# Second-layer experts by dispatch, with the routing inside the attention and all loops written out

## The chip, the cores and the metric

One core of a Trainium2 chip runs the whole program in a single launch. Five instruction streams work side by side and meet only at semaphores: TensorE (PE: matmuls and transposes), VectorE (DVE), ScalarE (ACT), GpSimd (POOL) and SyncE (SP), which issues the DMA transfers. The metric is the device time of one execution in microseconds; lower is better. All data is float32.

## The reference

Two transformer layers over x of 2 batches x 1024 tokens x 128 channels. Each layer is a gated attention and a gated feed-forward block, each behind a modulated layer norm. The parts that matter for the change are in the second layer:

```python
h = _layernorm(x) * (1 + ca) + sa
x = x + ga * _L1_attn_ref(h, Wq, Wk, Wv, Wo)       # linear attention, 16 heads of 32, sequences of 128
h = _layernorm(x) * (1 + cb) + sb
x = x + gb * _L1_ffn_ref(h, gate_w, w1, w2, w3)

def _L1_ffn_ref(x, gate_w, w1, w2, w3):            # E = 8 experts, 4 of them masked out, K = 2, H = 704
    logits = where(expert >= 4, -inf, xf @ gate_w.T)
    top_w, top_idx = top_k(softmax(logits), 2)
    cw[token, top_idx] = top_w / sum(top_w)
    h = silu(xf @ w1[e]) * (xf @ w3[e])            # for every expert e
    out = sum_e cw[:, e] * (h_e @ w2[e])
```

So four experts are live, and each token uses two of them. The first layer has another attention and 16 experts of hidden width 256 of which each token uses one. x lies in the core's own memory as `x_sb`, 16 tiles of 128 tokens x 128 channels.

## The kernel before

The program is a sequence of phases, each of which ends with all engines meeting: setup, `rwkv_phase` (first attention, eight chunk steps, to about 225 us), `expert_phase` (first experts, to about 358 us), `hla_phase` (second attention, to about 679 us), `swiglu_phase` (second experts, to the end). Within a phase each engine runs a hand-written order of instructions, and semaphore counts tie the engines together.

`rwkv_phase`, `expert_phase`, `hla_phase` and `swiglu_phase` each hold a hardware loop (`Fori`) on every engine: three passes of two chunk steps in the first; four rounds of eight slot tiles in the second; six chunks in the third (`steps`, L1289 to L1300: chunk 0 and chunk 7 are written out beside the loop); four groups of 512 tokens in two loop passes or rounds in the fourth.

The first layer's experts go by dispatch. The token rows are written into slots sorted by expert (POOL's indirect DMA, L1010), SP reads 32 expert numbers into registers with `value_load` (L965) and fetches each slot tile's weights; the results go to DRAM (`slots_out`, L977) and POOL gathers them back (L1017).

`hla_phase` works in 64 units: 8 chunks of 128 tokens x 2 batches x 4 groups of heads. Per unit PE projects q, k, v (L1323 to L1325), transposes (L1338, L1339, L1343), and runs many 32-row products (L1361 to L1424); DVE makes `h_aT` (L1496), updates the state (L1499) and masks the products (L1505); ACT evicts. Every fourth unit carries an output projection. POOL adds the gated output into `x_sb` (L1521, L1524).

`swiglu_phase` starts when the attention is done. A preamble computes the layer norm, the transposed tokens, the logits, the softmax (ACT L1699), the top two (DVE L1754, L1757) and the weights of all tokens. Then all four experts are computed for every token: per group of 512 tokens 22 units (a block of 128 hidden channels of one expert, or two tails of 64), each of two up products (L1659, L1661), ACT's silu (L1716), DVE's product (L1784) and one down product (L1669). A token that doesn't use an expert enters it with weight zero: POOL scales the rows (L1811), PE transposes them (L1645), and these scaled tokens are the input of the w3 product. The result is transposed back (L1688), multiplied by the gate (L1788), added to `x_sb` (L1827) and stored from there (L1835).

## Time and profile before

| | us |
|---|---|
| median of 3 runs | 972.87 |
| lowest and highest | 969.47 and 982.83 |
| the profiled execution | 969.88 |
| its span in the trace | 968.1 |
| PE busy in it | 771.0 |
| DVE busy | 403.2 |
| ACT busy | 296.2 |
| POOL busy | 185.3 |

The profile is one execution on the core. A timeline row gives start and length in us, engine, line of the kernel, operation, output<-inputs, and in brackets the engine's idle time ahead of the row with what ended it; "issue" means that it waited for nothing that the profile shows. A float32 matmul appears as two entries (two passes), so a row with x4 holds two matmuls of the program. PEclk is the TensorE clock that was granted, as a share of full speed. Starts of matmuls are measured, their ends are modelled: the distance from one start to the next is the safer price.

### The profile page before, as it was taken

The numbers are of one execution on the slowest core, as the hardware profiler recorded it, in microseconds if no ns is written. First come the engines' busy times: TensorE is split into PE (matmuls) and PEld (weight loads), VectorE is DVE, ScalarE is ACT, GpSimd is POOL, SyncE is SP. The second block draws the span as 40 slices with busy tenths as digits, with TensorE's granted clock in tenths as the row PEclk, the third lists the DMA queues.
The fourth block names the chain that finished last, engine by engine and source line by source line (L and its number), as shares of the span: only waits on it lengthen the run. The fifth ranks groups of instructions, "written<-read, shape, count | busy, mean of one in ns | idle before, by whom it ended". The sixth has DMA issues, their size and how long they took to land. (4 is left out here: it accounts for less than half of the span.)

```text
span 968.1 us, 25870 instructions
## 1 busy us (share of the span) xinstructions
PE 771.0 (80%) x10310; PEld 542.1 (56%) x10310; DVE 403.2 (42%) x1126; ACT 296.2 (31%) x903; POOL 185.3 (19%) x285
## 2 busy tenths in 40 slices
PE   4777777744178329999898988999459999999997
PEld 4455555434067318887787877887424444444442
DVE  4366777752222254453443534444522222222221
ACT  0343444321034114443343333443122222322221
POOL 1245445431500350000000100000221010110100
PEclk8587878755579759999999999999559999999999
DMA  5700000002356200000000000000000000000000
GB/s 141 223 3 2 0 0 0 0 2 88 123 160 220 86 21 3 3 4 3 4 3 3 3 4 4 3 3 3 1 0 1 0 12 0 12 0 0 11 0 11
DMA packets 27296, 28.11 MB, mean 29 GB/s; under 512 B 3200, under 2 KB 20288, under 8 KB 27200
## 3 DMA queue, kind: packets, MB, share of 16 engines
q1 hardware_dynamic: 26176, 24.58, 8.2%
q0 software_dynamic: 1024, 2.10, 0.7%
q8 instruction: 79, 1.29, 0.6%
q14 instruction: 17, 0.14, 0.0%
HBM read 20.38 MB, written 6.29 MB: 28 GB/s over the span
## 5 line engine op out<-in xcount | busy, mean ns | idle before, releaser
L1505 DVE TENSOR_TENSOR h_masked<-quad,const 128x1536 f32<-128x1536 f32 (+2 forms) x66 | 112.8, 1709 | 141.7 <-PE quad L1367 134.6
L1659 PE MATMUL quad<-f_xg,moe_w 128*128 128x512 f32 x320 | 152.5, 602 | 0.8 <-ACT f_xg L1704 0.8
L1784 DVE TENSOR_TENSOR f_h<-f_sa,quad 128x512 f32<-128x512 f32 x88 | 60.6, 688 | 181.1 <-PE quad L1659 164.8
L1659 PEld LDWEIGHTS quad<-f_xg,moe_w 128*128 128x128 f32 x320 | 60.2, 193 | 70.0 <-issue 69.5
L1716 ACT ACTIVATE f_sa<-quad 128x512 f32<-128x512 f32 x88 | 52.5, 597 | 143.8 <-PE quad L1659 126.7
L1669 PE MATMUL bank<-f_h,moe_w 128*128 128x512 f32 x160 | 82.5, 597 | 0.0
L1521 POOL TENSOR_TENSOR h_added<-h_added,mod_row 128x128 f32<-128x128 f32 x16 | 7.3, 455 | 285.0 <-ACT h_added L1472 285.0
L1669 PEld LDWEIGHTS bank<-f_h,moe_w 128*128 128x128 f32 x160 | 29.7, 190 | 40.9 <-issue 40.9
L1476 ACT ACTIVATE h_gT<-bank 128x128 f32<-128x128 f32 x64 | 17.7, 277 | 113.9 <-PE bank L1410 112.4
L1361 PE MATMUL quad<-h_qk 32*128 32x128 f32 x1024 | 48.9, 307 | 0.0
L1323 PE MATMUL pair<-h_hT,hla_wq 128*128 128x128 f32 x128 | 32.0, 333 | 20.1 <-issue 16.4
L1452 ACT ACTIVATE h_qk<-pair 128x256 f32<-128x256 f32 x64 | 24.5, 383 | 71.3 <-PE pair L1325 71.3
L1361 PEld LDWEIGHTS quad<-h_qk 32*128 32x128 f32 x1024 | 36.1, 194 | 10.4 <-issue 8.6
L1811 POOL TENSOR_TENSOR g_hs<-g_h_all,g_cw 128x512 f32 (+1 forms) x20 | 20.6, 1040 | 93.2 <-PE pair L1645 71.8
L631 POOL TENSOR_TENSOR kl<-kl,tot 128x128 f32<-128x128 f32 x56 | 26.9, 481 | 45.1 <-DVE state L575 17.2
L1827 POOL TENSOR_TENSOR x_sb<-x_sb,f_gated 128x512 f32 x4 | 5.1, 1265 | 155.9 <-DVE f_gated L1788 155.9
L1323 PEld LDWEIGHTS pair<-h_hT,hla_wq 128*128 128x128 f32 x128 | 19.6, 192 | 24.5 <-issue 18.1
L1496 DVE TENSOR_TENSOR h_aT<-bank,const 128x128 f32<-128x128 f32 x64 | 18.7, 291 | 31.7 <-PE bank L1424 29.1
L1381 PE MATMUL bank<-h_qk,h_state 32*32 32x128 f32 x512 | 28.1, 291 | 0.0
L1402 PE MATMUL bank<-h_masked,h_vt 128*32 128x128 f32 x512 | 27.8, 290 | 0.0
L1017 POOL DMA_INDIRECT e_yt<-slots_out,slot_of_token x16 | 15.6, 976 | 63.0 <-DMA slots_out<-e_yg 58.4
L1224 PE MATMUL quad<-const,h_all 128*128 128x128 f32 x16 | 4.0, 423 | 29.5 <-DVE h_all L1153 29.5
(285 smaller groups left out, 1673.5 us busy)
## 6 DMA issues: line engine op xcount, KB each, us to landing
e_w<-in_experts_dram SPq DMA_DIRECT2D x32, 257.5 KB
moe_w<-in_moe_w_dram SPq DMA_DIRECT2D x2, 1408.0 KB, 9.3
slots_in<-zero SPq DMA_DIRECT2D x4, 512.0 KB, 4.0
e_xg<-slots_in SPq DMA_DIRECT2D x8, 256.0 KB, 3.2
slots_out<-e_yg SPq DMA_DIRECT2D x8, 256.0 KB, 4.6
moe_w<-in_moe_w_dram SPq DMA_DIRECT2D x4, 320.0 KB, 7.2
x_sb<-in_L_attn_x_dram SPq DMA_DIRECT2D x2, 512.0 KB, 8.4
out_dram<-x_sb SPq DMA_DIRECT2D x4, 256.0 KB, 2.4
```

The costliest lines, as they stand in the source:

```text
L631: pool.tensor_tensor(halves(kl[m + 1], m)[:, :, 0], halves(kl[m], m)[:, :, 0], per(tot[m], m)[:, :, 1:2].to_broadcast([P, N >> (m + 1), 1 ...
L1323: pe.matmul(proj[:, 0:P], W["q"][:, cols], hT[b][:, :], start=True, stop=True)
L1361: last = pe.matmul(quad[:, h, a * P:(a + 1) * P], qk[q][head(h), 1 - a, :], qk[q][head(h), a, :], start=True, stop=True, tile_position=(h ...
L1381: pe.matmul(left[head(h), 0:P], states[k][head(h), 2 * D:3 * D], qk[k][head(h), 1, :], start=True, stop=False, tile_position=(h * D, h * D ...
L1402: last = pe.matmul(left[head(h), 0:P], vt[k][:, head(h)], new[:, h, P:2 * P], start=False, stop=True, tile_position=(0, h * D), skip_group ...
L1452: act.activation(qk[q][:, :, :], proj[:, 0:2 * P].rearrange("p (k n) -> p k n", k=2), ACT.Copy).then_inc(s_qkv, 1)
L1505: dve.tensor_tensor(masked[k % 4][:, :, a * P:z * P], quad[:, :, a * P:z * P], cst("causal")[:, None, a * P:z * P].to_broadcast([P, HPG, ( ...
L1659: return pe.matmul(dst[:, :], w[:, e, f * P:(f + 1) * P], src(e), start=True, stop=True)
L1669: pe.matmul(acc[b][:, :], w, hh[n % 2][:, :], start=(n == 0), stop=(n == U - 1))\
L1716: act.activation(sa[n % 2][:, :], up_a[n % 2][:, :], ACT.Silu).then_inc(s_sa, 1)
L1784: dve.tensor_tensor(hh[n % 2][:, :], sa[n % 2][:, :], up_b[n % 2][:, :], ALU.mult)\
L1811: pool.tensor_tensor(hs[k % 2][:, :, :], h_all[:, bass.ds(at + k, 1), :].to_broadcast([P, E, C]), cw[:, 0, bass.ds(at + k, 1), :].rearrang ...
```

## The change

1. `hla_phase` and `swiglu_phase` become one `layer1_phase`. The second layer's experts are computed only for the tokens that use them. Each token's row is written to two slots (`moe1_slots` in DRAM, one region for each expert). A row is a payload of 132 numbers: 128 channels of the normalised token, the token's number, the weight, the batch and a spare. 4096 rows in four regions fill at most 35 tiles of 128 slots.
2. The routing of chunk m runs inside the attention on its way through chunks m + 1 and m + 2, one part a unit (`routed`): DVE's stats, centre, normalise, logits, top2, ranked, slots and weights; two 8-column matmuls on PE (`rank`); an Exp on ACT (`weigh`); POOL's deviation, logit products, payload copy and four indirect scatters (`send`). There are two payload buffers, used in turn. Chunk 7's routing comes after the attention. Its gate rows are made ahead of the attention: a load, matmuls on PE, a copy on ACT.
3. SP stores each finished chunk of `x_sb` to a DRAM accumulator `moe1_acc`.
4. DVE computes from the four counts the tables `expert_of` and `row_of`; PE reads 35 expert offsets into registers, once; SP reads 5 row numbers a round.
5. Seven rounds of five tiles. A tile: SP loads 128 payload rows; PE transposes them, three up products (512, 512 and 384 columns: w1 and w3 side by side), six transposes of the hidden rows, six down products of 128 columns, with w addressed through the register; ACT three silus and two copies; DVE three products, a copy and the weighting; POOL picks the gate row by batch (three operations) and scatters with an add into `moe1_acc`. Each scatter waits until the one before it has landed.
6. At the end SP copies 1 MB from `moe1_acc` to the output.
7. In the phases of layer 0 and in the attention the hardware loops are replaced by loops that are written out when the program is built. A fill of `moe1_slots` (4.5 MB, constant) and another layout of the expert weights are loaded during `rwkv_phase`.

The diff, cut to its core:

```diff
-            with eng.Fori(0, CHUNKS - 2) as n:
+            for n in range(0, CHUNKS - 3):
                 for k in range(PER):
-                    step(n + 1, k)
+                    step(n + 2, k)
...
+        def routed(i, k, at):
+            if k % PER != at:
+                return None
+            m = i + k // PER - (1 if at >= 3 else 2)
+            return m if not isinstance(m, int) or m >= 0 else None
...
+            def rank(m, first):
+                pe.wait_ge(r_ohs, m + 1)
+                pe.wait_ge(r_cum, m * 2 + 1)
+                pe.matmul(right[:, 232:240], cst("before"), ohs[:, :, :]...
+                pe.matmul(right[:, 232:240], cst("ones"), cum[:, :, :]...
...
+            def expert(n):
+                return pe.value_load(expert_of[0:1, bass.ds(n, 1)], min_val=0, max_val=(E - 1) * EXPERT1)
+            turn(0, 0)
+            experts = [expert(n) for n in range(TILES1)]
+            ups(0, 0, 0, experts[0])
...
+            def down(i, k, e):
+                pe.wait_ge(f_mostc, tile(i, k) + 2)
+                pe.wait_ge(f_restc, tile(i, k) + 2)
+                pe.wait_ge(f_y, tile(i, k) + (1 if k else 2))
+                for f in range(FULL1):
+                    pe.matmul(acc[k % 2], hidT[k][:, f * P:(f + 1) * P],
+                              W2[:, bass.ds(e + (2 * F1 + f * C), C)], start=(f == 0), stop=False)
...
+            def round_(i, last):
+                for k in R:
+                    ups(i, k, 2, es[k])
+                    turn_most(i, k)
+                    turn(*((i, k + 2) if k + 2 < U else (i + 1, k + 2 - U)))
+                    ups(j, q, 0, es[k + 1])
+                    turn_rest(i, k)
+                    ups(j, q, 1, es[k + 1])
+                    down(i, k, es[k])
...
+            def step(i, k):                                             # VectorE
+                dve.tensor_tensor(aT[q][:, :], right[:, 0:P], ...
+                m = routed(i, k, 2)
+                if m is not None:
+                    ranked(m)
+                dve.scalar_tensor_tensor(out=states[q][:, :], ...
+                if m is not None:
+                    slots(m)
+                    weights(m)
+                for at, part in ((3, stats), (4, centre), (5, normalise), (7, logits), (0, top2)):
+                    m = routed(i, k, at)
+                    if m is not None:
+                        part(m)
+                dve.tensor_tensor(masked[k % 4][:, :, a * P:z * P], ...
...
+            def scatter(i, k):
+                pool.wait_ge(f_y, n + 2)
+                pool.wait_ge(f_add, n * 16)
+                pool.indirect_dma_start(out=t["moe1_acc"], ..., in_=yg[k][:, :], compute_op=ALU.add)\
+                    .then_inc(f_add, 16)
...
+            sp.wait_ge(f_add, 16 * TILES1 + 16)
+            sp.dma_start(out..., t["moe1_acc"][0:BATCH * SEQ, :]...).then_inc(f_out, 16)
```

DVE's order in the attention before, at the head of the loop (L1295 is the loop's own): `h_aT`, `h_state` and `h_masked` follow each other, with nothing between them but the loop's register arithmetic.

```order
L1295 UNCONDITIONAL_BRANCH
L1295 ISA
L1496 TENSOR_TENSOR h_aT<-bank,const 128x128
L1499 SCALAR_TENSOR_TENSOR h_state<-h_state,bank 128x96
L1504 REGISTER_ALU
L1505 TENSOR_TENSOR h_masked<-quad,const 128x1536
L1495 REGISTER_ALU
```

The same place now, the unit of a chunk that holds `top2`, from the end of the unit ahead of it:

```order
L1829 TENSOR_TENSOR h_aT<-bank,const 128x128
L1835 SCALAR_TENSOR_TENSOR h_state<-h_state,bank 128x96
L1781 MAX g_mx<-g_lg 128x8 x2
L1785 MAX_INDEX g_idx<-g_mx,g_lg 128x8 x2
L1786 TENSOR_TENSOR g_gap<-g_mx 128x2
L1788 CAST g_idf<-g_idx 128x4
L1790 TENSOR_TENSOR g_oh<-const,g_idf 128x16
L1794 TENSOR_TENSOR g_ohs<-g_oh 128x8
L1796 TENSOR_TENSOR g_cum<-g_cum,g_ohs 128x4
L1848 TENSOR_TENSOR h_masked<-quad,const 128x1536
```

Nine instructions (MAX and MAX_INDEX are two each) have moved in between the state and the mask; two units later the unit with `ranked`, `slots` and `weights` holds seven more, of which the first stands between `h_aT` and `h_state`.

PE's order in the second layer's experts before, at the head of the loop: up products of 512 tokens and one down product per block of 128 hidden channels.

```order
L1651 UNCONDITIONAL_BRANCH
L1651 ISA
L1654 ISA
L1674 ISA
L1659 MATMUL quad<-f_xg,moe_w 128x512 x2
L1674 REGISTER_ALU
L1659 MATMUL quad<-f_xg,moe_w 128x512 x2
L1668 REGISTER_ALU
L1669 MATMUL bank<-f_h,moe_w 128x512
```

PE's order there now, from chunk 7's rank and the counts (`g_cum`) over the first transposed tile of payload rows (`f_xg`) to the first of 35 register loads:

```order
L1513 MATMUL bank<-g_cum,const 128x8
L1566 MATMUL bank<-g_cum,const 128x4
L1585 MATMUL pair<-const,f_xg 128x128
L1625 TENSOR_LOAD g_expert_of
L1625 ISA x2
```

and the middle of one tile (`h_masked` is the memory that now holds the hidden rows; ISA rows are register arithmetic for an address):

```order
L1593 ISA
L1593 MATMUL quad<-moe_w,f_xT 128x384
L1601 MATMUL quad<-const,h_masked 128x128 x4
L1585 MATMUL pair<-const,f_xg 128x128
L1593 ISA
L1593 MATMUL quad<-moe_w,f_xT 128x512
L1608 MATMUL pair<-const,h_masked 128x128 x2
L1593 ISA
L1593 MATMUL quad<-moe_w,f_xT 128x512
L1617 ISA
```

followed by the six down products, each behind an ISA row of its own. The loads stand behind a transpose that waits for the first payload tile, and seven transposes of 128 columns stand among three wide products.

## Rows read from the trace of the kernel before

**Rows 1.** Windows: PE, PEld, DVE, ACT, POOL busy us (x), granted clock, DMA share, GB/s
```profile
50.00:150.00 100.00, 76.92 (x1017) 52.14 (x1015) 69.26 (x253) 39.72 (x133) 48.54 (x82) 0.83 0.00 1
...
500.00:680.00 180.00, 165.76 (x4074) 143.49 (x4066) 78.23 (x103) 66.15 (x257) 12.18 (x27) 0.97 0.01 3
680.00:700.00 20.00, 9.68 (x46) 9.34 (x47) 13.29 (x65) 2.39 (x4) 5.15 (x8) 0.53 0.01 1
...
720.00:840.00 120.00, 118.65 (x313) 51.35 (x311) 30.98 (x45) 31.59 (x53) 8.53 (x9) 0.99 0.01 3
```

**Rows 2.** Timeline of PE, second experts: the first product, and three rows in the middle
```profile
716.85 1.22 PE L1659 MATMUL quad<-f_xg,moe_w 128*128 128x512 f32 x1 [0.76 <-ACT f_xg L1704]
...
880.32 1.88 PE L1659 MATMUL quad<-f_xg,moe_w 128*128 128x512 f32 x4
882.04 1.02 PE L1669 MATMUL bank<-f_h,moe_w 128*128 128x512 f32 x2
```

**Rows 3.** Timeline of PE: first and last of five loop edges in the attention
```profile
437.82 0.37 PE L1323 MATMUL pair<-h_hT,hla_wq 128*128 128x128 f32 x1 [3.05 <-issue]
...
601.11 0.37 PE L1323 MATMUL pair<-h_hT,hla_wq 128*128 128x128 f32 x1 [3.53 <-issue]
```

**Rows 4.** Timeline of DVE in the attention, the mask of three units in a row
```profile
622.80 1.76 DVE L1505 TENSOR_TENSOR h_masked<-quad,const 128x1536 f32<-128x1536 f32 x1 [1.61 <-PE quad L1367]
...
627.06 1.76 DVE L1505 TENSOR_TENSOR h_masked<-quad,const 128x1536 f32<-128x1536 f32 x1 [1.61 <-PE quad L1367]
...
632.22 1.76 DVE L1505 TENSOR_TENSOR h_masked<-quad,const 128x1536 f32<-128x1536 f32 x1 [2.51 <-PE quad L1367]
```

**Rows 5.** Timeline of PE, first layer: the same transpose in four steps
```profile
105.35 0.44 PE L743 MATMUL quad<-const,xn 128*128 128x128 f32 x2 [2.48 <-DVE xn L448]
...
126.98 0.44 PE L743 MATMUL quad<-const,xn 128*128 128x128 f32 x2 [2.53 <-DVE xn L448]
...
149.69 0.44 PE L743 MATMUL quad<-const,xn 128*128 128x128 f32 x2 [2.48 <-DVE xn L448]
```

**Rows 6.** Timeline of PE: 128-column matmuls late and at the start of the attention
```profile
601.43 0.39 PE L1324 MATMUL pair<-h_hT,hla_wk 128*128 128x128 f32 x2
601.65 0.39 PE L1325 MATMUL pair<-hla_wv,h_hT 128*128 128x128 f32 x2
...
360.60 0.64 PE L1324 MATMUL pair<-h_hT,hla_wk 128*128 128x128 f32 x2
361.03 0.64 PE L1325 MATMUL pair<-hla_wv,h_hT 128*128 128x128 f32 x2
```

**Rows 7.** Timeline of POOL: the last write of the attention into x_sb
```profile
678.39 0.45 POOL L1524 TENSOR_TENSOR x_sb<-x_sb,h_added 128x128 f32<-128x128 f32 x1
```

**Rows 8.** Value loads: DVE's table, SP's first load after it, and line 965 by source
```profile
248.82 0.17 DVE L1107 TENSOR_SCALAR expert_of_tile<-r_te 1x32 int32<-1x32 f32 x1
...
254.03 4.62 SPq L969 DMA_DIRECT2D e_w<-in_experts_dram  x8
...
L965 SPq TENSOR_LOAD <-expert_of_tile x32: 261/263/677, 249.0 to 305.8; - x32
```

**Rows 9.** Timelines of POOL and SP: the last two scatters, and the load behind them
```profile
266.42 0.96 POOL L1010 DMA_INDIRECT slots_in<-h_all,slot_of_token  x1 [0.31 <-issue]
267.69 0.96 POOL L1010 DMA_INDIRECT slots_in<-h_all,slot_of_token  x1 [0.30 <-issue]
...
269.93 6.89 SPq L973 DMA_DIRECT2D e_xg<-slots_in  x3
```

**Rows 10.** Page, parts 6 and 3: DRAM transfers to landing, and instruction fetch
```profile
slots_out<-e_yg SPq DMA_DIRECT2D x8, 256.0 KB, 4.6
...
out_dram<-x_sb SPq DMA_DIRECT2D x4, 256.0 KB, 2.4
...
q8 instruction: 79, 1.29, 0.6%
```

**Rows 11.** Page, part 5: the product on DVE in the last stage
```profile
L1784 DVE TENSOR_TENSOR f_h<-f_sa,quad 128x512 f32<-128x512 f32 x88 | 60.6, 688 | 181.1 <-PE quad L1659 164.8
```

More of the change, by code:

```diff
@@ L428, in steps @@
             step(0, 0, True, False)
-            with eng.Fori(0, CHUNKS // 2 - 1) as j:
+            for j in range(0, CHUNKS // 2 - 1):
                 step(j * 2 + 1, 1, True, True)
@@ L985, in _ @@
                 load_x(s, 0)
-            with sp.Fori(0, ROUNDS - 1) as i:
+            for i in range(0, ROUNDS - 1):
                 experts = experts_of(i + 1)
@@ L1036, in _ @@
                 act.sem_inc(s_out[s], 16)
-            with act.Fori(0, ROUNDS) as i:
+            for i in range(0, ROUNDS):
                 for k in range(DEPTH):
@@ L1113, in _ @@
             dve.wait_ge(s_exp, 3)
-            with dve.Fori(0, ROUNDS) as i:
+            for i in range(0, ROUNDS):
                 def inputs(half):
@@ L1184, in _ @@
                       stop=True).then_inc(s_rank, 1)
-            with pe.Fori(0, ROUNDS) as i:
+            for i in range(0, ROUNDS):
                 def transposes(half):
@@ L1441, in _ @@
             steps(pe, step)
+            pe.wait_ge(r_place, (CHUNKS - 2) * 2 + 1)
+            rank(CHUNKS - 1, True)
+            pe.wait_ge(r_cum, CHUNKS * 2)
+            pe.matmul(left[:, 256:256 + E], cst("ones"), cum[:, 0, :], start=True, stop=True).then_inc(s_cnt, 1)
+            pe.wait_ge(s_w2, 16 * S_W2)
+            pe.wait_ge(r_place, (CHUNKS - 1) * 2 + 1)
+            pe.sem_inc(f_hh, 3)
+            pe.sem_inc(f_mostc, 1)
+            pe.sem_inc(f_restc, 1)
+            pe.sem_inc(f_y, 2)
@@ new lines, in turn_most, with turn_rest @@
+            def turn_most(i, k):
+                pe.wait_ge(f_hh, tile(i, k) * 3 + 5)
+                pe.wait_ge(f_mostc, tile(i, k) + 1)
+                for f in range(4):
+                    last = pe.transpose(most[:, f * P:(f + 1) * P], hh[k][:, f * P:(f + 1) * P], cst("ident"))
+                last.then_inc(f_most, 1)
+            def turn_rest(i, k):
+                pe.wait_ge(f_hh, tile(i, k) * 3 + 6)
+                pe.wait_ge(f_restc, tile(i, k) + 1)
+                for f in range(2):
+                    last = pe.transpose(rest[:, f * P:(f + 1) * P], hh[k][:, (4 + f) * P:(5 + f) * P], cst("ident"))
+                last.then_inc(f_rest, 1)
@@ new lines, in _ @@
+            dve.wait_ge(s_tab, 10)
+            dve.scalar_tensor_tensor(out=rt[:, :], in0=te[:, :], scalar=float(CAP1 // P), in1=bt[:, :], op0=ALU.mult,
+                                     op1=ALU.subtract).then_inc(s_tab, 1)
+            dve.wait_ge(s_tab, 11)
+            dve.tensor_tensor(rt[:, :], rt[:, :], cst("iota35")[0:1, :], ALU.add).then_inc(s_tab, 1)
+            dve.wait_ge(s_tab, 12)
+            dve.tensor_scalar(row_of[:, :], rt[:, :], float(P), None, ALU.mult).then_inc(s_table, 1)
@@ new lines, in round_ @@
+            def round_(i, last):
+                for k in R:
+                    hidden(i, k, 2)
+                    j, q = (i, k + 1) if k + 1 < U else (i + 1, 0)
+                    keep_rest(i, k)
+                    if not last or k + 1 < U:
+                        hidden(j, q, 0)
+                        hidden(j, q, 1)
+                    result(i, k)
+            hidden(0, 0, 0)
+            hidden(0, 0, 1)
+            round_(0, False)
+            for n in range(0, ROUNDS - 2):
+                round_(n + 1, False)
@@ new lines, in _, with chunk @@
+            pool.wait_ge(s_growc, 1)
+            pool.wait_ge(s_fill, 16)
+            pool.dma_start(t["moe1_acc"][BATCH * SEQ:BATCH * SEQ + P, :], blank[:, 0:C]).then_inc(f_add, 16)
+            def chunk(i, first=2, last=False):
+                if first >= 1:
+                    add(i - 1, 1)
+                if not last:
+                    pool.wait_ge(s_proj, i * PER + GROUPS)
+                    fetch(i + 1, 0)
+                if first >= 2:
+                    send(i - 2)
+                if first >= 1:
+                    deviation(i - 1)
+                    products(i - 1)
+                    payload(i - 1)
+                add(i, 0)
+                if not last:
+                    pool.wait_ge(s_proj, i * PER + 2 * GROUPS)
+                    fetch(i + 1, 1)
```

696 lines of the change are left out of this document (418 added, 278 removed).

## The prediction

> **What bounds the kernel now.** I read the windows first, to see which engine is full in which stretch. In the second attention PE is busy 165.8 of 180 us at a granted clock of 0.97, and in the second experts 118.7 of 120 at 0.99, while no other engine is busy for half of the time [rows 1]. PE is the bound of both stages. Between them, 680 to 700, it is busy half of the time at the lower level: there the span is set by the preamble's chain. Next I read PE's timeline of the experts: two up products (x4) start 1.72 us before what follows, so a pass of 512 columns costs 0.43 us and a matmul 0.86 [rows 2]. This stage runs from 716.85 to the end, 251.3 us. The preamble lasts from the last write into x_sb, which ends at 678.84 [rows 7], to 716.85: 38.0 us. Last, PE's timeline of the attention. PE stood idle 3.05 and 3.53 us, for "issue", ahead of the first and the last of five loop edges [rows 3]; nothing that the profile shows was awaited.
>
> **The attention's loop edges.** From the first edge to the last are four passes in 163.3 us, 40.8 each [rows 3]. Without an edge a chunk is six units of 4.26 and two with the output projection of 5.16, by the distances of DVE's masks [rows 4]: 35.9. So an edge costs 4.9: the idle 3 to 3.5, and a slower unit behind it. Five edges: **-24.7**. The instruction fetch moved 1.29 MB in all [rows 10]; at 64 bytes each, my assumption, that is about PE's 20,000 entries, so the loop's body was already fetched pass by pass, and writing it out needs no more of it per us.
>
> **The first layer's loops.** One transpose starts at 105.35, 126.98 and 149.69: 21.63 without and 22.71 with an edge between [rows 5], so 1.1 for each of three edges, **-3.2**. The first experts' rounds have three edges too; no row isolates one there. Bounds 0 and 5 us, I take 1 each: **-3**. The 4.5 MB fill is issued early in the first layer, where nothing waits for DMA (DMA share 0.00) [rows 1]; if that cover went, it is about 15 us at the 2 MB in 6.6 that the zero fill of the first experts needs by its issues; I cost it at nothing.
>
> **Gate rows ahead of the attention.** A small load that lands in about 2.4 [rows 10], four matmuls at the lower clock and an ACT copy come before PE's first projection: **+4** (bounds 2 and 7).
>
> **Routing in the attention.** PE gains two logical matmuls of 8 columns a chunk with their waits; their cost is at most that of two 128-column ones, 0.22 each at full clock [rows 6]: +3.5. ACT must change its table for the first Exp; no table load is in the rows, bounds 0.3 and 3, I take 1.3. On DVE the nine instructions of top2 are the longest insertion, 0.17 each by the shortest DVE row [rows 8] and up to 0.25, so 1.5 to 2.2. They stand ahead of a mask that waits 1.61 us for PE, 2.51 in units with the projection [rows 4]. That covers almost all. What is late if not is the mask, then the products behind it; the state and `h_aT` follow. I take +1 in all, and 0 and 12 as bounds: 12 is 0.2 of a us in each of 60 units. Sum of this part **+5.8**. POOL's five operations and four sends a chunk, under 12 us, lie in 36 us of a POOL that was busy 12.2 of 180 [rows 1].
>
> **From the attention's end to the first up product.** Chunk 7's routing is serial: some 30 dependent DVE, POOL, PE and ACT operations of 0.17 [rows 8] to 0.45 [rows 7], 9.4 us. Then four sends 1.27 apart [rows 9]; the last is issued at 13.3. The last scatter of the first layer was issued at 267.69 and the load that needs all of them at 269.93 [rows 9], so it landed within 2.24: 15.5. The load of the first payload tiles and its landing, 2.4 to 4.6 for larger ones [rows 10]: 19. On PE the transpose of that tile stands ahead of the 35 register loads, so they start only then. SP read eight in the 5.0 us from the table (248.99) to its first load (254.03) [rows 8]: 0.62 each, of which TENSOR_LOAD is 0.26. 35 x 0.62 = 21.7. First up product at 41 instead of 38.0: **+3** (bounds -10, if PE reads in 0.26, and +6).
>
> **The tiles.** Per tile PE runs 1408 columns of up products, 2.35 us by 0.86 per 512 [rows 2]; seven transposes, one pass each, at 0.11, 0.77; six down products of two passes, 1.34 [rows 6]. Together 4.46 us. The nine address instructions have no row on PE. Lower bound 0 each (they are read ahead), upper bound 0.15, about half of what a value load costs beside its TENSOR_LOAD [rows 8]; I take 0.05, nearest to the loop's register arithmetic, which stood between products that followed at 0.43 a pass [rows 2]. So 4.9 a tile, 35 tiles 171.5. DVE's three products of 192 to 256 columns are at most half of 0.69 each [rows 11], with copy and weighting under 1.9; ACT about 2; POOL three of 0.45 [rows 7] and 0.96 [rows 9]: none comes near 4.9. Beyond that 3 at the lower clock after the 21 us of loads, 4 to fill and for stray bubbles, and 11 for the end: weighting, scatter to landing (3), and the 1 MB copy (7; bounds 3 and 12 from 4.6 and 2.4 for a quarter of it [rows 10]). 189.5 against 251.3: **-61.8**.
>
> This needs the full clock. In the attention, which has three transposes a unit, 0.97 was granted; in the first layer, with PE busy 76.9 of 100 us, 0.83 [rows 1]. At 0.83 a tile is 4.46 / 0.83 + 0.44 = 5.8, and the run is 31 us longer. I keep 4.9, because the tiles keep PE as busy as the attention does. The Trainium skill speaks against that: TensorE: Matmul & The Clock Gate, Part 4, says that the clock gate doesn't engage for transposes, since they don't count as PE-busy in the same way. By that rule seven transposes, 0.77 of each tile's 4.9 us, would not count, and the tile would be as the one at 0.83; the attention's rows don't show such an effect.
>
> **The sum.** 968.1 - 24.7 - 3.2 - 3 + 4 + 5.8 + 3 - 61.8 = 888.2 of span. The profiled execution was 969.88, 1.8 above its span, and the median of the runs 3.0 above that: 890 to 893, so **892 us**.
>
> **The rivals.**
> - *Lower clock in the tiles*, as just worked out: 5.8 a tile, 923 us. If PE stays at the lower level altogether, as between 680 and 700 (0.53) [rows 1], a tile is 8.9 and the run 140 longer, about 1030. Against it: PE has work queued throughout. 0.12 and 0.04.
> - *The chain of scatters*. Each waits for the landing of the one before it. A plain scatter takes up to 2.24 to land [rows 9]. With the add its target must be read too: 2.24 + 2.4 = 4.6 hides in 4.9. With the 4.6 of a write to DRAM [rows 10] plus about 1, 5.6 a tile: 35 x 0.7 = 25 more, 916 us. 0.18.
> - *The other side: scatters with add above 7.2*. The rest of the change saves 18, and the tiles with start and end may take 251 + 18, so the run is slower than before from (269 - 18) / 35 = 7.2 a tile, and over 2% slower from 7.7. It needs an add that goes row by row; at 9 it is 1035 us. Nothing in the rows speaks for it but that no accumulating transfer is among them. 0.06.
> - *Register-addressed matmuls bound by PE's sequencer*: at 0.15 for each address and another 0.07 for the second pass's, 5.8 to 6.5 a tile, 923 to 948 us. 0.15.
> - *The dispatch gives nothing and only the edges count*: its tiles at 7, gains 20: about 955. 0.04.
>
> **How the numbers follow.** My forecast (4.5 to 5.3 a tile) gets 0.41. It spans 862 (4.46 a tile and cheap loads) to 908. The range of all goes to 946, which takes in the scatter chain, the clock at 0.83 and most of the sequencer's case, and leaves out about 0.17. A measurement of this kernel can tell about 2% from no change, 19 us, so faster means below 953: 0.41 + 0.12 + 0.18 + 0.15 = 0.86. Slower is 0.04 + 0.06 = 0.10. The last case, at 950 or a little more, is the 0.04 for the same.
>
> **What would show it.** Attention: no idle "issue" ahead of projections, chunks of 36 to 37 us; if DVE binds, PE waits for the mask. Preamble: 35 loads on PE in about 21.7 us. Tiles: down products of successive tiles 4.9 apart with a granted clock near 1. If scatters bind, POOL's come evenly and PE waits for a copy behind `f_y`. If addresses bind, PE idles between down products with nothing awaited. The end: one copy of about 7 us. I would be wrong above all if a tile is not 4.9: each 0.1 is 3.5 us.

## The result

| | before | changed |
|---|---|---|
| median, us | 971.25 (4 runs) | 940.51 (4 runs) |
| lowest and highest | 969.47 and 982.83 | 932.72 and 945.68 |
| profiled execution | 969.88 | 932.72 |
| its span | 968.1 | 930.9 |

The ratio of the changed kernel to the kernel before is 0.965, with a 95% interval from 0.955 to 0.976. So the change makes the kernel 31 us faster. I had forecast 892, which is 81 us faster than the median of 972.87 known then. The direction was right, and 940.51 still lies in the range of 862 to 946, but the gain is 31 us and not 81. Medians here and below are over all executions; two of the kernels below have one execution over 1.5% above their fastest (`e5_fill_split` 935.36, `e9_lazy_loads` 922.76), and without it their medians are 922.02 and 907.17. The stages of the two profiled executions show where it went:

| stage | before | changed | difference | forecast |
|---|---|---|---|---|
| start to the attention's first projection | 360.1 | 375.0 | +14.8 | -2.2 |
| attention, to the end of its last write to x_sb | 318.7 | 326.6 | +7.8 | -18.9 |
| from there to the first up product | 38.0 | 42.0 | +4.0 | +3 |
| second experts, to the end | 251.3 | 187.4 | -63.9 | -61.8 |
| span | 968.1 | 930.9 | -37.2 | -79.9 |

The part of the prediction on the new stages, the last two rows, is within about 2 us in each. The part on the old stages, in which loops were written out and some work was put in, is 44 us off.

First the windows of the changed kernel's profile, with the columns of [rows 1]: most of the first layer's attention, the second attention, and the second experts.

```profile
50.00:200.00 150.00, 119.96 (x1466) 80.69 (x1466) 95.74 (x349) 54.42 (x182) 67.51 (x117) 0.72 0.06 13
374.00:702.00 328.00, 314.28 (x7260) 268.28 (x7260) 174.88 (x384) 123.25 (x472) 73.61 (x113) 0.96 0.04 11
743.00:920.00 177.00, 174.99 (x874) 113.25 (x874) 65.77 (x175) 65.03 (x174) 88.28 (x136) 0.99 0.19 25
```

The reader should see three things. The experts run at a granted clock of 0.99, and PE is busy for 99% of the time. POOL is busy for half of the time there, where it was busy for 7% in the second experts before [rows 1], and doesn't bind. The first layer's attention was granted 0.72 from 50 to 200, where the kernel before was granted 0.82 in the same window.

The tiles, in the timelines of PE and of POOL: the down products of two tiles in a row, and the scatters of these tiles.

```profile
908.52 1.34 PE L1617 MATMUL bank<-moe_w,h_masked 128*128 x10
...
909.79 0.48 PE L1620 MATMUL bank<-moe_w,h_masked 64*128 x2
...
910.21 0.91 PE L1593 MATMUL quad<-moe_w,f_xT 128*128 x2
910.96 0.60 PE L1601 MATMUL quad<-const,h_masked 128*128 128x128 f32 x4
...
913.34 1.34 PE L1617 MATMUL bank<-moe_w,h_masked 128*128 x10
```

```profile
911.40 1.60 POOL L2050 DMA_INDIRECT moe_acc<-f_y,f_token  x1 [2.25 <-DVE f_y L1916]
...
916.22 1.57 POOL L2050 DMA_INDIRECT moe_acc<-f_y,f_token  x1 [2.13 <-DVE f_y L1916]
```

These two are 4.82 apart; in the middle of the stage a tile takes 4.92, by PE's transposes (L1585):

```profile
803.07 0.27 PE L1585 MATMUL pair<-const,f_xg 128*128 128x128 f32 x1
808.00 0.27 PE L1585 MATMUL pair<-const,f_xg 128*128 128x128 f32 x1
```

POOL waits over 2 us ahead of each scatter, for DVE's result of this tile and not for the scatter ahead. The last scatter with add and the copy of 1 MB to the output stand in the list of DMA issues of the last 13 us (the last number is us from issue to landing). The median of all 35 scatters is 3.3, so the chain of scatters has room within 4.92:

```profile
moe_acc<-f_y,f_token POOLq DMA_INDIRECT x1, 3.2
out_dram<-moe_acc SPq DMA_DIRECT2D x1, 5.1
```

The attention. Each chunk from the third on has one unit of 7.4 to 9.2 us, where a unit takes 4.26 [rows 4]. Here is the fourth of the six, around 587. First PE, then POOL, ACT and DVE, each on its own timeline.

```profile
582.38 0.49 PE L1429 MATMUL pair<-h_hT,hla_wq 128*128 128x128 f32 x2
...
587.36 0.24 PE L1545 MATMUL bank<-h_vt,h_kqt 128*32 128x32 f32 x8
...
588.09 0.39 PE L1431 MATMUL pair<-hla_wv,h_hT 128*128 128x128 f32 x2
...
590.44 0.58 PE L1473 MATMUL quad<-h_aT,h_qk 32*128 32x128 f32 x8 [0.65 <-DVE h_aT L1829]
```

```profile
587.30 1.10 POOL L1980 DMA_INDIRECT moe_slots<-g_pay,g_slot  x1 [0.17 <-issue]
588.70 0.97 POOL L1980 DMA_INDIRECT moe_slots<-g_pay,g_slot  x1 [0.30 <-issue]
589.98 0.96 POOL L1980 DMA_INDIRECT moe_slots<-g_pay,g_slot  x1 [0.30 <-issue]
591.24 0.96 POOL L1980 DMA_INDIRECT moe_slots<-g_pay,g_slot  x1 [0.30 <-issue]
```

```profile
591.55 0.38 ACT L1664 ACTIVATE h_qk<-pair 128x256 f32<-128x256 f32 x1 [3.82 <-DMA slots_in<-zero]
```

```profile
590.10 0.29 DVE L1829 TENSOR_TENSOR h_aT<-bank,const 128x128 f32<-128x128 f32 x1 [2.86 <-remote]
...
593.18 1.76 DVE L1848 TENSOR_TENSOR h_masked<-quad,const 128x1536 f32<-128x1536 f32 x1 [1.89 <-remote]
```

DVE's `h_aT` waits for PE's L1545, which by its row was over at 587.60. DVE starts at 590.10. ACT waits for L1431, over at 588.48, and starts at 591.55. So up to there PE's matmuls stand in the trace at their usual distances, but those who wait for PE start 2.5 to 3.1 us late. (The names of the releasers there, a DMA of an earlier phase and "remote", are those of semaphores used again; they are not to be trusted.) It begins with POOL's four payload scatters and ends with them. PE itself then waits, for `h_aT` first, and behind that three times for "issue", 0.17, 0.42 and 0.34 us; all six long units have such waits at the same place, and `e3_loads_first` below, which has no long unit, has none. As the ends of matmuls are modelled, the trace can't tell whether PE's signals come late or the work behind them. The next projection is at 595.97, 8.4 us behind the one at 587.54.

The second stretch that I missed, the first layer's attention: the same transpose as in [rows 5] in two pairs of steps, and PE's longest wait for issue between the first two.

```profile
40.18 0.41 PE L766 MATMUL quad<-const,xn 128*128 128x128 f32 x2 [1.52 <-DVE xn L471]
...
48.36 0.49 PE L819 MATMUL pair<-rl,kl 64*32 64x32 f32 x29 [2.69 <-issue]
...
63.68 0.41 PE L766 MATMUL quad<-const,xn 128*128 128x128 f32 x2 [2.19 <-DVE xn L471]
...
130.88 0.41 PE L766 MATMUL quad<-const,xn 128*128 128x128 f32 x2 [2.42 <-DVE xn L471]
...
157.01 0.49 PE L766 MATMUL quad<-const,xn 128*128 128x128 f32 x2 [2.19 <-DVE xn L471]
```

The second step, 40.18 to 63.68, takes 23.5 us; before it took 18.6 (42.43 to 61.06). The sixth, from 130.88, takes 26.1 where [rows 5] has 21.6 and 22.7. From the first transpose of these steps to the eighth are 155.7 us, against 146.0 before; 4.9 of the 9.7 more stand in the second step, 6.8 in the five behind it, and the first is 2.0 shorter.

Between attention and experts the chain is as forecast, with the loads one block:

```profile
701.08 0.45 POOL L1949 TENSOR_TENSOR x_sb<-x_sb,h_added 128x128 f32<-128x128 f32 x1
```

```profile
720.17 0.47 PE L1585 MATMUL pair<-const,f_xg 128*128 128x128 f32 x1 [8.99 <-DMA f_xg<-moe_slots]
743.50 2.07 PE L1593 MATMUL quad<-moe_w,f_xT 128*128 x2 [22.85 <-issue]
```

### The profile page after: what moved, and what is told of

Read it like the earlier page. It is cut to its first block, busy times and chain, and to the rows that moved or that the text cites. A ratio compares the mean times of both kernels' runs of the same rounds, so it can differ in the third digit from the quotient of the medians.

```text
span 930.9 us, 26177 instructions
## 1 busy us (share of the span) xinstructions
PE 719.1 (77%) x10523; PEld 555.1 (60%) x10523; DVE 431.1 (46%) x1331; ACT 289.4 (31%) x967; POOL 306.2 (33%) x476
## 4 chain that ended last, share of the span: by engine, by line
PE 50%; issue 4%; DVE 2%; another core or an unknown queue 2%; DMA 1%; POOL 1%; ACT 0%; POOLq 0%; SPq 0%; DVEq 0%; PEldq 0%
PE quad L1593 10%; PE bank L1617 4%; PE quad L1467 4%; PE bank L1493 3%; PE pair L1429 3%; PE bank L1487 3%; PE bank L1520 2%; PE quad L1473 2%; PE quad L1601 2%; PE pair L1454 2%; PE bank L1620 2%; PE pair L1430 2%; PE pair L1431 2%; PE bank L1525 2%; PE bank L1537 2%
## 5 line engine op out<-in xcount | busy, mean ns | idle before, releaser
L1593 PE MATMUL quad<-moe_w,f_xT 128*128 x210 | 105.5, 585 | 22.9 <-issue 22.9
L2050 POOL DMA_INDIRECT moe_acc<-f_y,f_token x35 | 55.6, 1589 | 108.4 <-DVE f_y L1916 105.9
L1904 DVE TENSOR_TENSOR h_masked<-f_sa,quad 128x256 f32<-128x256 f32 (+1 forms) x105 | 41.5, 395 | 80.2 <-ACT f_sa L1712 80.2
L1712 ACT ACTIVATE f_sa<-quad 128x256 f32<-128x256 f32 (+1 forms) x105 | 38.4, 366 | 127.0 <-PE quad L1593 121.2
L1617 PEld LDWEIGHTS bank<-moe_w,h_masked 128*128 128x128 f32 x350 | 41.7, 191 | 22.2 <-issue 22.2
L1593 PEld LDWEIGHTS quad<-moe_w,f_xT 128*128 128x128 f32 x210 | 32.4, 194 | 28.9 <-issue 24.8
L1617 PE MATMUL bank<-moe_w,h_masked 128*128 x350 | 47.1, 281 | 0.7 <-DVE h_masked L1908 0.7
L1467 PEld LDWEIGHTS quad<-h_qk 32*128 32x128 f32 x1024 | 36.2, 187 | 10.7 <-issue 8.7
L1829 DVE TENSOR_TENSOR h_aT<-bank,const 128x128 f32<-128x128 f32 x64 | 18.6, 291 | 48.5 <-PE bank L1545 30.5
L1980 POOL DMA_INDIRECT moe_slots<-g_pay,g_slot x32 | 32.1, 1003 | 11.0 <-issue 8.7
L2039 POOL TENSOR_TENSOR f_gsel<-f_gdiff,f_xg 128x128 f32<-128x128 f32 x35 | 33.3, 952 | 0.0
L614 POOL TENSOR_TENSOR xx<-xx,hT 128x256 f32<-128x256 f32 x40 | 24.3, 636 | 16.4 <-DVE xx L487 16.4
```

The costliest lines, as they stand in the source:

```text
L1467: last = pe.matmul(quad[:, h, a * P:(a + 1) * P], qk[q][head(h), 1 - a, :], qk[q][head(h), a, :], start=True, stop=True, tile_position=(h ...
L1593: pe.matmul(up[u][:, 0:w], xT[k][:, :], W2[:, bass.ds(e + u * 4 * P, w)], start=True, stop=True).then_inc(f_up, 1)
L1617: pe.matmul(acc[k % 2], hidT[k][:, f * P:(f + 1) * P], W2[:, bass.ds(e + (2 * F1 + f * C), C)], start=(f == 0), stop=False)
L1712: act.activation(sa[u][:, 0:WIDTH[u]], up[u][:, 0:WIDTH[u]], ACT.Silu).then_inc(f_sa, 1)
L1904: dve.tensor_tensor(hh[k][:, at:at + w], sa[u][:, 0:w], up[u][:, w:2 * w], ALU.mult).then_inc(f_hh, 1)
L1980: pool.indirect_dma_start(out=t["moe1_slots"], out_offset=bass.IndirectOffsetOnAxis(ap=slot[:, b * 2 + k:b * 2 + k + 1], axis=0), in_=pay[ ...
```

## The experiments

The runs fell on two chips, which I call chip 1 and chip 2; the chip of the first result is not known. The kernel before takes about the same on both (970.26 to 973.13 us on chip 1, 973.48 on chip 2). Stage times are from each run's profiled execution, as above. "Attention" is from the first projection to the end of the last write to `x_sb`, 318.7 in the kernel before and 326.6 in the changed kernel.

### Does the burst of scatters hold up PE?

`e1_no_send` leaves out the scatters of chunks 0 to 5, so most tiles compute on blank rows. The waits for these scatters are left out too (not shown).

```diff
-                for b in range(BATCH):
+                for b in range(BATCH if m >= CHUNKS - 2 else 0):
```

> Leaves out the payload scatters of chunks 0 to 5 (24 of 32 indirect DMAs of POOL in the attention; the tiles then compute on blank rows). In the changed kernel one unit of every chunk from chunk 2 on takes 7.4 to 9.2 us instead of 4.26, and it begins when POOL issues its four scatters. Theory A (the scatters hold up PE's semaphores or work): these six units go back to 4.26 to 5, the attention gets 25 to 28 us shorter, the run is about 905 to 915. Rival B (instruction fetch for the written-out code, or SP's 64 KB store of the chunk that starts at the same time): the units stay at 7.4 to 9.2 and the run within 5 us of the changed kernel.

`e2_spread` keeps all four and issues them one at a time, between POOL's other work of the chunk.

```diff
-                    send(i - 2)
+                    send(i - 2, (0,))
                 deviation(i - 1)
+                    pool.wait_ge(s_proj, i * PER + 7)
+                    send(i - 2, (1,))
                 products(i - 1)
                 payload(i - 1)
+                    send(i - 2, (2,))
                 add(i, 0) ... fetch(i + 1, 1)
                 ...
+                    send(i - 2, (3,))
```

> The same scatters, but one each in units 3, 4, 6 and 8 of a chunk instead of four in a row. Theory A1 (only a burst of scatters holds PE up, a single one finds slack): the long units shrink to under 5 us and the run is 20 to 28 us faster than the changed kernel, about 912 to 920. Theory A2 (each scatter costs PE about 1.2 us wherever it stands): four units a chunk of about 5.4, the sum stays, run within 5 us of the changed kernel. Rival B as before: one unit a chunk stays at 7.4 to 9.2.

On chip 2 the first took 910.85 us (909.23 to 914.12) and the second 912.51 (902.18 to 914.56), and neither has a long unit: the attention is 298.7 and 298.6. That looked like theory A. But two other kernels measured with them, `e3_loads_first` and `e4_rwkv_loop` (below), keep the burst of four and have no long unit either. Their attention is 298.7 and 298.1. PE's projections there, in `e3_loads_first`, and the burst beside them:

```profile
570.30 0.49 PE L1429 MATMUL pair<-h_hT,hla_wq 128*128 128x128 f32 x2
574.56 0.49 PE L1429 MATMUL pair<-h_hT,hla_wq 128*128 128x128 f32 x2
```

```profile
570.05 1.10 POOL L1980 DMA_INDIRECT moe_slots<-g_pay,g_slot  x1 [0.17 <-issue]
571.46 0.97 POOL L1980 DMA_INDIRECT moe_slots<-g_pay,g_slot  x1 [0.30 <-issue]
572.73 0.96 POOL L1980 DMA_INDIRECT moe_slots<-g_pay,g_slot  x1 [0.30 <-issue]
```

The same burst at the same place of the unit, and the unit takes 4.26. So these four runs couldn't tell what the burst does in the changed kernel. I ran that again, unchanged.

> The changed kernel itself, unchanged, in more executions and perhaps on another chip. Of four variants, three kept its bursts of scatters or its written-out code as they were and none had a long unit in the attention. Theory A (a burst of four scatters holds PE up by itself) then needs the long units back here: about 933 to 945 us. Theory E (the hold-up isn't of the program but of the execution or the chip): no long units, attention about 300 us instead of 326.6, and 905 to 920 us. Theory F (the exact placement of the program matters, which every edit shifts): the long units come back here and in no variant.

On chip 1: 940.47 us (938.02 to 944.61), six long units of 7.0 to 9.4, attention 326.4. Theory E or F was left: the chip or the occasion, or the placement of the program. The next pair decided it.

> The changed kernel once more, beside the variant with the loads first, on one chip. So far all bursts with long units ran on one chip (and on the unknown one of the first result), and the bursts without long units on another. Theory E (the chip decides): both kernels of this pair, which have the same bursts, behave alike: both have long units (attention about 327 us), or neither has (about 299). Theory F (the placement of the program decides): this one has them, the other doesn't, whatever the chip.

> The other of the pair: the loads ahead of the first transpose, bursts as in the changed kernel. Theory E: as its partner, with or without long units. Theory F: no long units while its partner has them.

Both fell on chip 1. The changed kernel took 939.85 and has the long units, attention 327.8. `e3_again`, the very kernel that had none on chip 2, took 931.43 and has them too: six of 8.2 to 9.1, attention 326.6. Theory E: it is not the program's placement. All runs on chip 2 were made on one occasion, so the chip itself and that occasion aren't told apart; on chip 1 the burst had its long units on all three occasions. One more pair, on chip 1 again, asks whether the burst is needed there.

> One scatter each in four units instead of four in a row, and nothing else. On the chip where the changed kernel has its long units: if a burst is what it takes (theory A1), none of 7 to 9 us is left and the attention takes 299 instead of 327; if each scatter costs its share (A2), four units a chunk are 1 us longer. On a chip without long units it tells nothing new: 299.

> Two bursts of two scatters a chunk, about two and a half units apart. If PE falls behind with every scatter that follows another one closely, each pair costs 1 to 2.5 us, together about half of the burst of four: attention about 312. If the slack of a unit covers a pair: 299. On a chip without long units: 299 either way.

`e8_pairs` is as `e2_spread`, with `send(i - 2, (0, 1))` behind the fetch and `send(i - 2, (2, 3))` behind the products. `e2_again` took 913.82 us: no long unit, attention 299.6. SP's store of each chunk (rival B) is still there, so it isn't the cause. `e8_pairs` took 924.35 in its one run, attention 308.4, where I expected 312. Its PE and POOL:

```profile
588.45 0.49 PE L1429 MATMUL pair<-h_hT,hla_wq 128*128 128x128 f32 x2
593.97 0.49 PE L1429 MATMUL pair<-h_hT,hla_wq 128*128 128x128 f32 x2
598.24 0.49 PE L1429 MATMUL pair<-h_hT,hla_wq 128*128 128x128 f32 x2
```

```profile
588.19 1.07 POOL L1981 DMA_INDIRECT moe_slots<-g_pay,g_slot  x1 [0.16 <-issue]
589.57 0.97 POOL L1981 DMA_INDIRECT moe_slots<-g_pay,g_slot  x1 [0.30 <-issue]
```

The unit with the pair takes 5.52, the next 4.27. The chunk's second pair falls into a unit with an output projection, which takes 5.62 to 5.65 instead of 5.16. So on chip 1 a scatter that stands alone costs PE nothing, a pair 1.3 or 0.5 us, and four in a row 3 to 5. On chip 2 four in a row cost nothing. What differs between the two, and what in the chip makes those who wait for PE start late, these runs don't show. PE's waits for "issue" in the long units leave the supply of its instructions as one untested candidate.

### What lengthens the first layer's attention?

`e5_fill_split` cuts the fill of the slots (8576 packets of 528 bytes, the 4.5 MB of the change's list) into seven DMAs, one behind each step. POOL's wait for the fill is adapted (not shown).

```diff
-            sp.dma_start(t["moe1_slots"].rearrange("(q p) n -> p q n", p=P),
-                         blank[:, None, :].to_broadcast([P, SLOTS1 // P, PAY])).then_inc(s_fill, 16)
+            rows = t["moe1_slots"].rearrange("(q p) n -> p q n", p=P)
+            for n in range(7):
+                a, z = n * 10, min(n * 10 + 10, SLOTS1 // P)
+                sp.wait_ge(s_state, 3 * (n + 1))
                 ...
+                sp.dma_start(rows[:, a:z, :], blank[:, None, :].to_broadcast([P, z - a, PAY])).then_inc(s_fill, 16)
```

> The 4.4 MB fill of the slots, which the changed kernel issues in one DMA at the start, is cut into seven pieces, one behind each step of the first layer's attention. In the changed kernel the second step took 23.5 us where the kernel before took 18.6, with 2.7 us in which PE waited for issue while the fill's packets ran. Theory G (the fill holds up PE's instruction fetch): the second step falls to 18 to 20, the run gets 3 to 5 us faster. Rival: the later steps each lose what the second gains, no difference.

Measured on chip 1 beside `after_again`: 925.07 us (920.78 to 935.36) against 940.47. The second step takes 18.4 instead of 27.4, by the same transposes:

```profile
43.64 0.66 PE L770 MATMUL quad<-const,xn 128*128 128x128 f32 x2 [1.50 <-DVE xn L475]
...
62.08 0.41 PE L770 MATMUL quad<-const,xn 128*128 128x128 f32 x2 [2.19 <-DVE xn L475]
```

PE's wait for issue is gone, and the later steps didn't lose it again: 146.7 us from first to eighth instead of 166.3. The other profiles say the same of the second step. All eleven with the whole fill have one wait for issue of 2.0 to 2.8 us while the fill's packets run, and a second step of 23.4 to 27.8 us; the four with the split fill have no such wait, and 18.4 to 18.8.

The gain of 15 is three times what I expected. Of the 19.6 us between the two profiles, 9.0 stand in the second step and 10.7 in the five behind it. Those go together with the clock: by the record of the granted clock, from the first of these steps to 20 us behind the start of the eighth, PE was at the lower of its two levels (1.2 of 2.4 GHz) for 76 us in `e5_fill_split` and for 132 in `after_again`; in the kernel before for 72, in the first result for 104. Over these four profiles the phase is the longer, the more of it is at the lower level: 146.7, 166.3, 146.0, 155.7. Part of that is chance: the three profiles of the unchanged new kernel have 155.7, 159.7 and 166.3. Which of the two, the longer steps or the lower clock, brings on the other isn't shown.

The transposes of the next five steps in `e5_fill_split`, which has no loop edge:

```profile
83.53 0.41 PE L770 MATMUL quad<-const,xn 128*128 128x128 f32 x2 [2.43 <-DVE xn L475]
...
106.24 0.41 PE L770 MATMUL quad<-const,xn 128*128 128x128 f32 x2 [2.43 <-DVE xn L475]
...
127.73 0.41 PE L770 MATMUL quad<-const,xn 128*128 128x128 f32 x2 [2.44 <-DVE xn L475]
...
150.34 0.41 PE L770 MATMUL quad<-const,xn 128*128 128x128 f32 x2 [2.43 <-DVE xn L475]
...
171.90 0.41 PE L770 MATMUL quad<-const,xn 128*128 128x128 f32 x2 [2.42 <-DVE xn L475]
```

From 62.08 on these are steps of 21.4, 22.7, 21.5, 22.6 and 21.6. The kernel before, with its loop, has 21.6, 22.7, 21.6, 22.7 and 21.6. So the alternation of 21.63 and 22.71, which I had read as a step without and a step with an edge [rows 5], is there without any edge. `e4_rwkv_loop` (next), with its edges at the same steps as the kernel before, has it the other way round: 22.8, 21.7, 22.8, 21.7, 22.7.

`e4_rwkv_loop` puts the hardware loop back in this phase alone, and `e6_three` and `e7_four` are a pair that differ by the same edit.

```diff
-            for j in range(0, CHUNKS // 2 - 1):
+            with eng.Fori(0, CHUNKS // 2 - 1) as j:
```

> Only the first layer's attention gets its hardware loop back. From its first to its eighth step the changed kernel took 155.7 us, the kernel before 146.0, where I had forecast 3 us less without the loop. Theory C (written-out code is slower there, through instruction fetch or the clock that its rhythm is granted): 146 to 149 and the run 7 to 10 us faster than the changed kernel. Rival D (the 4.4 MB fill of the slots in the second step, and chance in the granted clock): the second step stays near 23.5, the total stays at 152 to 158.

> Three edits together: the split fill, PE's register loads ahead of the first transpose, and the scatters spread over four units. If each gives what it gave or should give alone: 8 for the loads, 4 for the fill, and the spread scatters nothing where there are no long units, so about 12 us faster than the unchanged kernel on the same chip. If the gain of the fill is lost again in the granted clock: 8.

> As the three edits together, and with the hardware loop back in the first layer's attention. Theory C (written-out code costs 7 to 10 us there): 7 to 10 faster than the three edits alone. Rival D (the loop's edges cost the 1 us each that the trace of the kernel before shows, and the rest was the fill and the clock): 0 to 3 slower.

`e4_rwkv_loop` took 903.84 us on chip 2, with 156.2 in the phase and 26.1 in the second step: the fill's stall is there with the loop as without. The pair, on chip 1: 898.33 (896.03 to 901.93) and 891.40 (884.76 to 897.86), with 152.4 and 144.2 in the phase. That looks like 7 us for the loop. But 3.5 of the 8.2 us between the two phases stand in the first step (18.4 and 14.9), which is written out in both, and `e10_five`, below, has the loop and the split fill as `e7_four` has, and its phase took 151.3; `e5_fill_split`, written out, took 146.7. What the loop is worth is lost in the granted clock, and I leave it open. One hint remains for theory C: with the whole fill the five steps behind the second take 111.7 in `e4_rwkv_loop` and 117.1 to 120.6 in the ten written-out profiles, but it is one profile. My -3.2 for writing it out has no support.

`e6_three` has no long unit on chip 1 (attention 299.3), as `e2_again`. Against `after_again` it is 42 us faster where I expected 12, since I took the spread scatters to give nothing: 27 in the attention, 5 from the loads, the rest in the first layer.

### Where do the 35 register loads belong?

`e3_loads_first` moves the block of loads ahead of the first transpose.

```diff
-            turn(0, 0)
             experts = [expert(n) for n in range(TILES1)]
+            turn(0, 0)
             ups(0, 0, 0, experts[0])
```

> PE's 35 register loads stand ahead of the first transpose of a payload tile instead of behind it, so they begin with the table and run while the last scatters land and the first tile loads. In the changed kernel PE waited 9.0 us for that tile and then 22.9 for the loads. Expected: the first up product 7 to 9 us earlier, the run 7 to 9 us faster than the changed kernel (about 932), if the loads are the chain there. Rival: the loads slow down or wait for something else behind the table, under 2 us.

On chip 2 it took 897.44 us (896.07 to 909.40). The stage between attention and first up product is 37.3 in both its runs, against 42.0: 4.7 instead of the 7 to 9 expected. The loads now begin 13.2 us behind the attention, when the table is written, instead of 18.7 behind it; of PE's 9 us of waiting, 3.5 were for that table in any case, and the first transpose with its copy, nearly 1 us, now stands behind the loads. They are still the chain: 23 us in which nobody needs 32 of the 35. The run is 43 us faster than the first result, but only 4.7 of these come from the loads; most of the rest is that this chip had no long units. On chip 1 `e3_again` is 8.4 faster than `after_third` beside it, with two executions each, of which the stage explains 4.6.

`e9_lazy_loads` reads three offsets ahead and then one a tile.

```diff
-            experts = [expert(n) for n in range(TILES1)]
+            experts = [expert(n) for n in range(3)]
             turn(0, 0)
             ...
                     down(i, k, es[k])
+                    if len(experts) < TILES1:
+                        experts.append(expert(len(experts)))
```

> Only the first three expert offsets are read ahead; the others one a tile, behind its down products. In the changed kernel the 35 loads take 23 us of PE's sequencer, 0.65 each, with nothing in PE. If the sequencer's 0.65 is hidden behind matmuls that wait in the queue, the first up product comes 21 us earlier, tiles stay at 4.92, and the run is about 20 us faster than the changed kernel. If not, each tile gets up to 0.65 longer and the run is the same or 2 us slower.

On chip 1: 911.30 us (904.56 to 922.76), with the bursts and their long units in it. The first up product comes 19.7 us behind the attention instead of 42.0, and the tiles stay close to 4.92:

```profile
751.40 0.27 PE L1585 MATMUL pair<-const,f_xg 128*128 128x128 f32 x1
756.35 0.27 PE L1585 MATMUL pair<-const,f_xg 128*128 128x128 f32 x1
761.45 0.27 PE L1585 MATMUL pair<-const,f_xg 128*128 128x128 f32 x1
```

4.95 and 5.10, so of each load's 0.65 us 0.03 to 0.18 is left on the path; the mean tile is 5.00, which leaves 0.08. By the stages of the profiled execution that is 22 us less ahead of the tiles and 3 more from the first up product on, so 19 to 20 net, as expected. The medians differ by more, 911.30 against 940.47. The profiled execution is the slowest of the four; the others have no profile, so their gain beyond 20 isn't accounted for.

### All together

`e10_five` has the split fill, the spread scatters, the loop in the first layer's attention and the loads one a tile.

> The split fill, the spread scatters, the hardware loop of the first layer's attention and the one-a-tile loads together. The version with the loads in one block ahead of the first transpose took 891 median on the chip with long units. With hidden loads: 20 less in the block, about 872 to 876; with loads that aren't hidden: 890 to 893.

On chip 1: 876.38 us (873.55 to 877.01), a ratio of 0.898 to the kernel before with an interval from 0.892 to 0.905. The changed kernel took 940.47 on that chip (`after_again`, at another time), 64 us more. Attention 299.5, first up product 20.0 behind it, where `e7_four` has 37.2: the hidden loads give 17 there and not 20. The tiles are 4.92 to 5.09, 4.94 in the mean, so here a load leaves 0.02.

## Why the prediction was right and wrong

**The tiles: right in size, and one term by luck.** 4.46 of PE work and 0.05 for each address made 4.9; 4.92 was measured, at a granted clock of 0.99. The 35 tiles with start and end took 187.4 against 189.5. The 0.46 beyond 4.46 is not in the nine addresses. The rows above show where it stands: ten passes of the down products take 1.27 from 908.52 to 909.79, 0.15 more than at 0.112 each; the two passes with 64 rows take 0.42 up to 910.21, 0.2 more; and the product of 384 columns takes 0.75 up to 910.96, 0.1 more than at 0.86 per 512. The two products of 512 columns have an address each and take 0.86, as without. Each address instruction of the down products took 0.046 us on PE's sequencer, beside matmuls that go on at 0.11. So the term of 0.45 was right in sum, and its mechanism wasn't. The end took the 11 us forecast, from the last down product at 919.6 to 930.9: the 1 MB copy landed in 5.1 and not 7, and the rest took 2 more. What was shorter is the start, 3.9 us where I had 3 and 4. Seven transposes stand in each tile and 0.99 was granted. The rule of the Trainium skill that I had weighed (TensorE: Matmul & The Clock Gate, Part 4: the clock gate doesn't engage for transposes) has no effect that this trace shows. The scatter rival falls as well: 3.3 us to landing, under 4.92.

**The step to the first up product: right.** 42.0 against 41, and for the reasons given: the loads stand behind the first transpose, which starts 18.6 behind the attention (forecast 19), 0.65 each against the forecast 0.62.

**The loop edges in the attention: right, and hidden.** I had -24.7 for five edges and +5.8 for the routing, -18.9 in all, so 299.8. Without the long units the attention takes 298.1 to 299.6 in the eight profiles that have none (one of them without most scatters, `e1_no_send`). No projection waits 3 us for issue any more. DVE's insertions hide in the wait ahead of the mask; the unit with the `rank` matmuls takes 4.94 instead of 4.26, so a chunk takes 36.6 us, where I had given 36 to 37.

**The scatters in the attention: the step that failed most.** I wrote that POOL's operations and sends lie in 36 us of a POOL that is nearly idle, and put them at nothing. I had checked whether POOL has the time, and not what its transfers do to the engines beside it. On chip 1 and in the first result each burst of four lengthens its unit by 3 to 5 us, six times over, together 25, and on four of them the unit behind is 0.3 to 1.1 longer, with PE at the lower clock: 27 us in all. It was in none of my rivals. In the trace of the kernel before, POOL's scatters run while PE waits for them anyway, so no row could show it; I should have given it a bound instead of nothing.

**The first layer: wrong, in two terms.** The first is the fill, which I put at nothing. In the first result it goes with +4.9 us in the second step, where PE waits 2.7 us for issue; over the runs the wait is 2.0 to 2.8, and it goes away when the fill is split. That "nothing waits for DMA" there was no ground for nothing, since PE's own instructions come by DMA too: the page had a queue for them with 1.29 MB [rows 10]. That the fill holds up just this queue is my reading; the trace shows the wait for issue and no more. I had costed the fill at 15 us if its cover went, and then kept it out of the sum. The second is the -3.2 for three edges. It rested on the alternation of 21.63 and 22.71, which `e5_fill_split` has without a loop: its five steps behind the second take 109.8 us, those of the kernel before 110.3. Instead of -3.2 the phase became +9.7 in the first result. The 6.8 us more in the steps behind the second, and the swing up to the 166.3 of `after_again`, go with the granted clock; that a stall early in the phase brings the lower clock on is likely from the split fill and not shown.

**The rest of the start.** The first experts did gain: from the last of their scatters to the last of the rows gathered back are 76.0 us instead of 78.6, near the forecast of -3. From there to the attention's first projection are 19.0 instead of 13.8, +5.2 against a forecast of +4 for the gate rows: PE's wait for the gate's load is 4.1 us, then 1.9 for issue. Another 2.8, between the eighth step and the last of those scatters, has no term in the forecast, and I didn't test it.

## What to carry to other kernels

Work put on an idle engine isn't free because that engine has time: ask what its transfers share with the engine that binds, and issue indirect DMAs one at a time between other work instead of in a burst. A large fill in a phase "without DMA" can still hold up the engine that binds; cut it into pieces. Two step times that differ by a us aren't yet the price of a loop edge: look for the same difference where there is no edge. Registers that PE reads are best read one tile ahead in the stream of matmuls: a block of them is time on the path, the same loads between matmuls cost almost none.

## What the runs showed of the hardware

- Bursts of indirect scatters by POOL made those who wait for PE's semaphores start 2.5 to 3.1 us late in the first result. The same program had 326.6 us in the attention on one chip (`e3_again`) and 298.7 on another (`e3_loads_first`), the latter on one occasion only. An optimisation checked on one chip only may look worthless or too good.
- A 4.5 MB fill made PE wait 2.0 to 2.8 us for issue in each of eleven profiles, and cutting it in seven took the wait away in all four.
- A value load costs PE's sequencer 0.65 us, of which 0.08 (`e9_lazy_loads`) and 0.02 (`e10_five`) remained in the mean when matmuls were queued ahead of it.
- An indirect scatter with add of 128 rows of 512 bytes into DRAM landed in 3.3 us (median of 35), beside at most 2.24 for a plain one [rows 9].
